# A three-layer graph network kernel: in layer 0 GpSimd instead of VectorE copies the gather indices of a pair

## The chip, the cores and the metric

The kernel runs on one core of one Trainium2 chip. The metric is the device time of one execution in microseconds; lower is better. Three executions of the kernel before took 4489.26, 4493.26 and 4494.06 us, with a median of 4493.26.

## The reference

A layer norm with ReLU in front, three rounds of mean aggregation over a graph (GraphSAGE), and the input added at the end. There are 100000 nodes of 128 features and 150000 edges sorted by destination, 100000 of them from a node to itself. The widths are 128, 256, 256 and 128; all is float32.

```python
def sage(h, w_self, w_neigh, b):
    agg = segment_sum(h[src], dst) * inv_deg
    return h @ w_self + agg @ w_neigh + b
h = jnp.maximum(_layernorm(x), 0.0)
h = relu(sage(h, ws0, wn0, b0))
h = relu(sage(h, ws1, wn1, b1))
return x + sage(h, ws2, wn2, b2)
```

## The kernel before, in words

The nodes are cut into tiles of 128, two tiles are a pair, and there are 392 pairs (`PAIRS`). A node's own edge to itself is added directly. The other edges of a tile, at most 128, have been put into a table in a preparation of about 200 us: `slot_index` holds for each tile and partition the source row to fetch, `slot_node` the place of its destination within the tile. A tile's sum over edges is then one gather of 128 rows and one matmul with a selection matrix. If the table does not hold all edges a flag leads to a general path (`general`); with these inputs it is not taken.

Each layer is a software pipeline in which every engine has its own program, and pair n is at another stage on each. `pipeline(eng, step, total, lag)` (line 83) calls `step` once per pair. Inside a step `first.back(k)` is the pair k places before, and it works in that pair's buffers. Buffers loaded from memory have 4 slots (`SLOTS`), most others 2 halves. Engines wait for each other with counting semaphores, and each queue is worked off in order. The order of the work within a step is written out by hand.

Layer 0, by engine, at the step of pair n:

- SyncE (`layer0_transfers`, lines 454 to 465) loads the pair's own rows of x into `raw[slot][:, 0:2]` as soon as pair n-4 is normalized (`L0.normed`), and stores the results P and Q of pair n-9.
- VectorE (`layer0`, line 1013) begins with `copies_index(L0, first)` (lines 978 to 985). It copies the two index columns of pair n from `slot_index` to `gather_at[slot]`, and adds one to `L0.index_copied`. Behind it, for pair n-1, it waits for the own rows and for both gathers (lines 1018 and 1019) and takes the statistics of four tiles (line 1021), then the selection matrix `select` (1026). There follow `self_scale` (1035), the moments (1039), `cat_lo` of pair n-4 (1047), `hid_lo` of pair n-6 (1055), Q of pair n-8 (1065), `rstd` (1073), the sum of own row and neighbours `agg` of pair n-2 (1082), its degree (1084), `shift` of pair n-1 (1088), `inv_degree` (1092) and P of pair n-7 (1099).
- GpSimd (`gathers`, lines 561 to 573) waits until pair n-4 is normalized, which frees the buffer, and until `L0.index_copied` is n+1; then it issues two indirect DMAs (line 569) that fetch 128 rows of x each into `raw[slot][:, 2:4]`.
- ScalarE (`layer0`, line 635) normalizes pair n-2 (line 649: two tiles of own rows, two of neighbours, then `L0.normed`), scales `agg` of pair n-3 (657), takes the square root for pair n-1 (663), the ReLU of pair n-5 (671), and `cat_hi` and `hid_hi` (679, 686).
- TensorE (`layer0`, line 1231) does the product of pair n-7 with the weights of the next layer (12 matmuls with 512 columns, `ps_out`), the sum matmuls of pair n-2 (line 1253, 4 matmuls, `ps_agg`), the transposes of pair n-3 (line 1264, which wait for `agg_ready` and for `cat_lo` of the pair before), and the product of pair n-4 (12 matmuls with 256 columns, `ps_hid`). Products are three terms of high and low parts, in `product` (line 1222).

Layer 1 has the same shape with other widths: `copies_index(L1, first)` is in VectorE's step there too, with a wait on the gathers of the slot's last use. Layer 2 works on groups of three tiles.

The lines that put the copy and the gathers in their order are these:

```python
def gather(s):
    if s.has(SLOTS):
        pool.wait_ge(freed, s.back(SLOTS).n + 1)
    pool.wait_ge(layer.index_copied, s.n + 1)
    pool.sem_inc(pool_may_go, 1)
    for j in range(2):
        pool.indirect_dma_start(...)
```

Of the kernel before, what the change touches and what calls it, by code (L numbers as in the profile page):

```python
# [16 lines left out]
D = 128  # L17
H = 256
PAIR = 2 * P
SLOTS = 4  # L20
PAIRS = -(-N_NODES // (PAIR * SLOTS)) * SLOTS
# [48 lines left out]
def peeled(step, first, last, total, slots=SLOTS):  # L70

    for n in range(first, last):
        step(Step(n // slots, n % slots, total, False, slots))


def looped(eng, step, first_use, last_use, total, slots=SLOTS):

    with eng.Fori(first_use, last_use) as i:
        for slot in range(slots):
            step(Step(i, slot, total, True, slots))  # L80


def pipeline(eng, step, total, lag, rounds=2, slots=SLOTS):

    assert lag < rounds * slots and total % slots == 0
    peeled(step, 0, rounds * slots, total, slots)
    looped(eng, step, rounds, total // slots, total, slots)
    peeled(step, total, total + lag, total, slots)


def build(nc, x, src, dst, windows, ws0, wn0, b0, ws1, wn1, b1, ws2, wn2, b2, out):
# [4 lines left out]
    h0_sums = nc.dram_tensor("h0_sums", [N_ROWS, D], FP32).ap()  # L96
# [9 lines left out]
    with ExitStack() as ctx:  # L106
        def sb(name, shape, dt=FP32):
            return ctx.enter_context(nc.sbuf_tensor(name, shape, dt))

        def sem(name):  # L110
            return ctx.enter_context(nc.semaphore(name))
# [23 lines left out]
        slot_index = sb("slot_index", [P, TILES], I32)  # L135
# [61 lines left out]
        raw = [t[:, :].rearrange("p (j f) -> p j f", j=4) for t in loaded_rows]  # L197
# [13 lines left out]
        gather_at = [sb(f"gather_at{i}", [P, SHARED], I32) for i in range(SLOTS)]  # L211
# [81 lines left out]
        tables_ready = sem("tables_ready")  # L293
# [53 lines left out]
        pool_may_go = sem("pool_may_go")  # L347

        L0, L1, L2 = Layer(0), Layer(1), Layer(2)
# [150 lines left out]
        def _(pool):  # L500
# [12 lines left out]
            for c in range(CHUNKS):  # L513
                pool.indirect_dma_start(win_mem[0:TP, c * 2 * WIN:(c + 1) * 2 * WIN], None, windows,
                                        bass.IndirectOffsetOnAxis(row_index[:, c:c + 1], axis=0),
                                        bounds_check=ROWS - 1, oob_is_err=False).then_inc(win_gathered, 16)
# [3 lines left out]
            last_row = pool.snap(limit)  # L520

            def general(pass_no):
                table, sums, width = GENERAL[pass_no]
                with pool.If(pool.value_load(general_flag[0:1, 0:1], min_val=0, max_val=1) != 0):
# [33 lines left out]
                    if pass_no == 0:  # L558
                        pool.wait_ge(ge_index_set, 1)

            def gathers(layer, table, rows_in, freed, width):
                def gather(s):
                    if s.has(SLOTS):
# [5 lines that stand above are left out]
                        pool.indirect_dma_start(rows_in[s.slot][:, j, 0:width], None, table,  # L569
                                                bass.IndirectOffsetOnAxis(gather_at[s.slot][:, j:j + 1], axis=0),  # L570
                                                bounds_check=last_row, oob_is_err=False
                                                ).then_inc(layer.gathered[s.slot], 16)
                pipeline(pool, gather, PAIRS, 0)

            def triple_gathers(s):
# [5 lines left out]
                for j in range(SHARED):  # L581
# [2 lines left out]
                                            bounds_check=last_row, oob_is_err=False  # L584
                                            ).then_inc(L2.gathered[s.slot], 16)

            pool.wait_ge(flag_set, 1)
            pool.wait_ge(nbr_cleared, SLOTS + 3)
            raw_nbr = [t[:, 2:4, :] for t in raw]
            general(0)  # L590
            with pool.If(pool.value_load(general_flag[0:1, 0:1], min_val=0, max_val=1) != 0):
                gathers(L0, h0_sums, raw_nbr, L0.normed, D)
            with pool.Else():
                gathers(L0, x, raw_nbr, L0.normed, D)

            for q in range(SLOTS):
                pool.memset(nbr[q][:, :, :], 0.0).then_inc(nbr_cleared, 1)
# [1 line left out]
            all_stored(pool, L0.stored, 2 * SLOT_USES)  # L599
            general(1)  # L600
            gathers(L1, p_dram, nbr, L1.summed, H)
            all_stored(pool, L1.stored, 2 * SLOT_USES)
            general(2)
# [149 lines left out]
        def _(dve):  # L753
# [221 lines left out]
                                          op1=ALU.add).then_inc(ge_nodes_set, 1)  # L975
                        dve.wait_ge(ge_nodes_set, 2)

            def copies_index(layer, s):

                if not s.live():  # L980
                    return
                if layer is not L0 and s.has(SLOTS):
                    dve.wait_ge(layer.gathered[s.slot], s.use * 32)
                dve.tensor_copy(gather_at[s.slot][:, 0:2], slot_index[:, bass.ds(s.n * 2, 2)]  # L984
                                ).then_inc(layer.index_copied, 1)

            def nbr_lo_part(layer, s, tiles, width):

                if not s.live():
                    return  # L990
                dve.wait_ge(layer.nbr_hi_ready, s.n + 1)
                if s.has(2):
                    dve.wait_ge(layer.summed, s.back(2).n + 1)
                dve.tensor_tensor(nbr_lo[s.half][:, 0:tiles, 0:width], nbr[s.slot][:, 0:tiles, 0:width],
                                  nbr_hi[s.half][:, 0:tiles, 0:width].bitcast(FP32), ALU.subtract
                                  ).then_inc(layer.nbr_split, 1)

            def means(layer, s, width, added):

                dve.wait_ge(layer.summed, s.n + 1)  # L1000
                if s.has(2):
                    dve.wait_ge(layer.turned, s.back(2).n + 1)
                for j in range(2):
                    last = dve.scalar_tensor_tensor(agg[s.half][:, j, 0:width],
                                                    row_sums[s.slot][:, j * H:j * H + width],
                                                    inv_degree[:, bass.ds(s.n * 2 + j, 1)],
                                                    added[:, j, 0:width], op0=ALU.mult, op1=ALU.add)
                last.then_inc(layer.agg_ready, 1)
# [2 lines left out]


            def layer0(first):
                copies_index(L0, first)
                t = first.back(1)
                if t.live():

# [23 lines left out]
                t = first.back(4)  # L1041
# [7 lines left out]
                t = first.back(6)  # L1049
# [7 lines left out]
                t = first.back(8)  # L1057
# [12 lines left out]
                t = first.back(1)  # L1070
# [3 lines left out]
                s = first.back(2)  # L1074
# [18 lines left out]
                t = first.back(7)  # L1093
# [9 lines left out]
            dve.wait_ge(nbr_cleared, SLOTS + 3)  # L1103
            dve.wait_ge(bias_loaded, 32)
            pipeline(dve, layer0, PAIRS, 8, rounds=3)

            general(1)


            def layer1(first):  # L1110
                copies_index(L1, first)
                nbr_lo_part(L1, first.back(4), L1_SPLIT, H)
                s = first.back(5)
                t = s.back(2)
                if t.live():

                    dve.wait_ge(L1.hi_ready, t.n + 1)
                    if t.has(2):
                        dve.wait_ge(L1.dense_done, t.back(2).n + 1)
                    dve.scalar_tensor_tensor(hid_lo[t.half][:, :, :],  # L1120
                                             l1_turn[t.half].rearrange("p (k n) -> p k n", k=2), 0.0,
                                             hid_hi[t.half][:, :, :].bitcast(FP32), op0=ALU.max, op1=ALU.subtract
                                             ).then_inc(L1.lo_ready, 1)
                t = s.back(4)
                if t.live():

                    dve.wait_ge(L1.z_ready, t.n + 1)
                    if t.has(SLOTS):
                        dve.wait_ge(L1.stored[t.slot], t.use * 32)
                    for j in range(2):  # L1130
                        last = dve.scalar_tensor_tensor(y_out[t.slot][:, j, :], z_out[t.slot][:, j, :],
                                                        self_scale[:, bass.ds(t.n * 2 + j, 1)],
                                                        l1_out[t.half][:, j * H + D:(j + 1) * H],
                                                        op0=ALU.mult, op1=ALU.add)
                    last.then_inc(L1.rows_ready, 1)
                if s.live():
                    dve.wait_ge(L1.own_loaded[s.slot], (s.use + 1) * 16)
                    means(L1, s, H, own[s.slot])
            pipeline(dve, layer1, PAIRS, 9, rounds=4)

            general(2)
# [238 lines left out]
```

## Time and profile before

| what | us |
|---|---|
| median of three executions | 4493.26 |
| the profiled execution | 4493.25 |
| its span, first to last instruction | 4491.1 |
| layer 0's gathers, first to last start | 199.9 to 2227.8 |
| layer 1's gathers, first to last start | 2264.1 to 3619.6 |
| layer 2's gathers, first to last start | 3640.5 to 4480.2 |
| TensorE busy | 3625.5 (81%) |
| VectorE busy | 3607.8 (80%) |
| ScalarE busy | 3057.1 (68%) |
| GpSimd busy | 2237.8 (50%) |

The profile calls the engines PE (TensorE matmuls), PEld (TensorE's weight loads), DVE (VectorE), ACT (ScalarE), POOL (GpSimd) and SP (SyncE). L984 is line 984 of the kernel. "<-" behind a group's idle time names what ended it. An instruction's duration reaches from its start to its last write, and the next one on the same engine may start before that; so durations on one engine can add up to more than the time that they fill. PEclk is TensorE's granted clock as a share of its full speed.

### The profile page before, as it was taken

What the parts mean: (1) busy time and instruction counts of PE and PEld (TensorE: products, weight loads), DVE (VectorE), ACT (ScalarE), POOL (GpSimd) and SP (SyncE); (2) the same over time, 40 slices, a digit from 0 to 9 for tenths busy, and PEclk for the clock granted to TensorE, in tenths of its full rate; (3) what the DMA queues carried; (4) which work ended last, traced back from release to release, by engine and by line L of the source; (5) the groups of instructions that cost most, each with busy time, mean ns of one, the idle gap of its engine ahead of it and who ended that gap; (6) DMA issues with size and microseconds to landing.
All of it is one profiled execution on the core that took longest, in us unless ns stands there. A gap on an engine that the chain in (4) does not pass through costs nothing. (4 is left out here: it accounts for less than half of the span.)

```text
span 4491.1 us, 111206 instructions
## 1 busy us (share of the span) xinstructions
PE 3625.5 (81%) x22512; PEld 3234.4 (72%) x22512; DVE 3607.8 (80%) x12979; ACT 3057.1 (68%) x7987; POOL 2237.8 (50%) x2122
## 2 busy tenths in 40 slices
PE   0199999999999999999978788777787765666565
PEld 0188888888888888888867677677677755555555
DVE  7899999999999999999956666666666666666666
ACT  0188888888888888888756666666666656666665
POOL 0144444444444444444355555555555556666665
PEclk9999999999999999999989999999999976665666
DMA  1044444444444444444456666666666667777777
GB/s 47 14 133 138 137 140 138 139 137 138 139 140 137 140 138 139 138 138 141 133 161 189 189 187 188 188 194 185 188 190 190 190 193 214 218 215 215 214 217 205
DMA packets 1040429, 726.89 MB, mean 162 GB/s; under 512 B 102859, under 2 KB 1012307, under 8 KB 1040303
## 3 DMA queue, kind: packets, MB, share of 16 engines
q1 hardware_dynamic: 854418, 569.79, 41.9%
q0 software_dynamic: 80384, 104.91, 9.6%
q10 hardware_dynamic: 105600, 51.92, 3.9%
q14 instruction: 21, 0.17, 0.0%
q8 instruction: 6, 0.10, 0.0%
HBM read 451.43 MB, written 360.72 MB: 181 GB/s over the span
## 5 line engine op out<-in xcount | busy, mean ns | idle before, releaser
L569 POOL DMA_INDIRECT loaded_rows<-in_x,gather_at x784 | 910.2, 1161 | 1263.4 <-DVE gather_at L984 1121.5
L1227 PE MATMUL ps_out<-w_hi,hid_hi 128*128 128x512 f32 (+1 forms) x3136 | 1111.5, 354 | 272.5 <-DVE hid_lo L1120 104.1
L569 POOL DMA_INDIRECT layer_mem<-p_rows,gather_at x784 | 787.9, 1005 | 601.6 <-issue 215.6
L1227 PE MATMUL ps_out<-w_lo,hid_hi 128*128 128x512 f32 (+1 forms) x3136 | 1065.7, 340 | 0.0
L1227 PE MATMUL ps_out<-w_hi,hid_lo 128*128 128x512 f32 (+1 forms) x3136 | 1060.2, 338 | 0.0
L1227 PEld LDWEIGHTS ps_out<-w_hi,hid_hi 128*128 128x128 f32 x3136 | 601.4, 192 | 421.9 <-issue 235.2
L582 POOL DMA_INDIRECT layer_mem<-z_rows,gather_at x528 | 527.3, 999 | 333.3 <-issue 154.8
L1227 PEld LDWEIGHTS ps_out<-w_hi,hid_lo 128*128 128x128 f32 x3136 | 600.9, 192 | 64.6
L1227 PEld LDWEIGHTS ps_out<-w_lo,hid_hi 128*128 128x128 f32 x3136 | 602.6, 192 | 50.3
L1120 DVE SCALAR_TENSOR_TENSOR hid_lo<-ps_out,hid_hi 128x512 fp32r<-128x512 f32 x392 | 270.6, 690 | 427.5 <-ACT hid_hi L727 351.2
L738 ACT ACTIVATE layer_mem<-iota_row,triple_node 128x128 f32<-128x128 f32 x1056 | 345.9, 391 | 272.9 <-issue 168.7
L1227 PE MATMUL ps_hid<-cat_hi,w_hi 128*128 128x256 f32 x1568 | 476.7, 304 | 0.0
L1227 PE MATMUL ps_hid<-cat_hi,w_lo 128*128 128x256 f32 x1568 | 445.2, 284 | 0.0
L1227 PE MATMUL ps_hid<-cat_lo,w_hi 128*128 128x256 f32 x1568 | 444.5, 283 | 0.0
L679 ACT ACTIVATE cat_hi<-ps_turn 128x512 fp32r<-128x512 f32 x392 | 234.6, 599 | 289.8 <-PE ps_turn L1264 285.5
L718 ACT ACTIVATE layer_mem<-ps_out 128x256 f32<-128x256 f32 x392 | 150.0, 383 | 391.3 <-DMA y_rows<-layer_mem 164.4
L1021 DVE BATCH_NORM_STATS2 stats<-loaded_rows 128x6 f32<-128x128 f32 x1568 | 341.2, 280 | 31.8 <-issue 12.3
L649 ACT ACTIVATE h_own<-loaded_rows,shift,rstd 128x128 f32<-128x128 f32 x784 | 342.1, 484 | 24.3 <-DVE shift L1088 14.1
L649 ACT ACTIVATE h_nbr<-loaded_rows,shift,rstd 128x128 f32<-128x128 f32 x784 | 340.6, 482 | 0.0
L1065 DVE SCALAR_TENSOR_TENSOR layer_mem<-stored_rows,self_scale,ps_out 128x256 f32<-128x256 f32 x784 | 339.3, 474 | 0.1
L671 ACT ACTIVATE layer_mem<-ps_hid,b_col 128x256 f32<-128x256 f32 x784 | 321.5, 460 | 1.1 <-DVE hid_lo L1055 0.7
L727 ACT ACTIVATE hid_hi<-ps_out 128x512 fp32r<-128x512 f32 x392 | 233.0, 594 | 109.5 <-PE ps_out L1322 87.5
(158 smaller groups left out, 8963.6 us busy)
## 6 DMA issues: line engine op xcount, KB each, us to landing
p_rows<-stored_rows SPq DMA_DIRECT2D x392, 256.0 KB
q_rows<-layer_mem SPq DMA_DIRECT2D x392, 256.0 KB
loaded_rows<-q_rows SPq DMA_DIRECT2D x392, 256.0 KB
loaded_rows<-y_rows SPq DMA_DIRECT2D x264, 192.0 KB
layer_mem<-in_x SPq DMA_DIRECT2D x264, 192.0 KB
out_rows<-stored_rows ACTq DMA_DIRECT2D x264, 192.0 KB
loaded_rows<-in_x SPq DMA_DIRECT2D x392, 128.0 KB
z_rows<-layer_mem SPq DMA_DIRECT2D x392, 128.0 KB
```

The source lines that it names most:

```text
L569: pool.indirect_dma_start(rows_in[s.slot][:, j, 0:width], None, table, bass.IndirectOffsetOnAxis(gather_at[s.slot][:, j:j + 1], axis=0), b ...
L582: pool.indirect_dma_start(triple_rows_in[s.slot][:, j, :], None, z_dram, bass.IndirectOffsetOnAxis(gather_at[s.slot][:, j:j + 1], axis=0), ...
L649: last = act.activation(rows, raw[t.slot][:, j, :], ACT.Relu, bias=shift[t.half][:, j:j + 1], scale=rstd[t.half][:, j:j + 1])
L671: last = act.activation(h1[t.half][:, m, :], ps_hid[t.half][:, m * PAIR:(m + 1) * PAIR], ACT.Relu, bias=b0_col[:, m:m + 1])
L679: act.activation(cat_hi[t.half][:, :, :], ps_turn[:, :].rearrange("p (k n) -> p k n", k=2), ACT.Copy).then_inc(L0.hi_ready, 1)
L718: act.activation(z_out[t.slot][:, :, :], l1_out[t.half].rearrange("p (j f) -> p j f", j=2)[:, :, 0:D], ACT.Copy).then_inc(L1.z_ready, 1)
L727: act.activation(hid_hi[t.half][:, :, :], l1_turn[t.half].rearrange("p (k n) -> p k n", k=2), ACT.Relu).then_inc(L1.hi_ready, 1)
L738: last = act.activation(triple_distance[s.half][:, b, :], iota_row[:, :], ACT.Abs, scale=-1.0, bias=triple_node[:, bass.ds(s.n * (2 * SHAR ...
L1021: last = dve.bn_stats(stats[t.half][:, j, :], raw[t.slot][:, j, :])
L1065: last = dve.scalar_tensor_tensor(q_out[t.slot][:, j, :], p_out[t.slot][:, j, :], self_scale[:, bass.ds(t.n * 2 + j, 1)], ps_out[t.half][: ...
L1120: dve.scalar_tensor_tensor(hid_lo[t.half][:, :, :], l1_turn[t.half].rearrange("p (k n) -> p k n", k=2), 0.0, hid_hi[t.half][:, :, :].bitca ...
L1227: ins = nc.tensor.matmul(o, a, b, start=n == 0, stop=n == len(terms) - 1)
```

## The change

In layer 0 the index copy leaves VectorE's step. GpSimd gets a step of its own, `layer0_gathers`, in place of `gathers`. At the step of pair n it waits until the gathers of pair n-4 have landed (the last to read that slot's `gather_at`) and copies the two index columns of pair n. Then, for pair n-1, it waits until pair n-5 is normalized and until its own copy of pair n-1 is done, and issues the two gathers. As it now reads `slot_index` itself, it waits once for `tables_ready` ahead of all. `copies_index` remains for layer 1 alone. Nothing else differs.

```diff
+            def layer0_gathers(table):
+                def step(first):
+                    if first.live():
+                        if first.has(SLOTS):
+                            pool.wait_ge(L0.gathered[first.slot], first.use * 32)
+                        pool.tensor_copy(gather_at[first.slot][:, 0:2], slot_index[:, bass.ds(first.n * 2, 2)]
+                                         ).then_inc(L0.index_copied, 1)
+                    s = first.back(1)
+                    if s.live():
+                        if s.has(SLOTS):
+
+                            pool.wait_ge(L0.normed, s.back(SLOTS).n + 1)
+                        pool.wait_ge(L0.index_copied, s.n + 1)
+                        pool.sem_inc(pool_may_go, 1)
+                        for j in range(2):
+                            pool.indirect_dma_start(raw[s.slot][:, 2 + j, :], None, table,
+                                                    bass.IndirectOffsetOnAxis(gather_at[s.slot][:, j:j + 1], axis=0),
+                                                    bounds_check=last_row, oob_is_err=False
+                                                    ).then_inc(L0.gathered[s.slot], 16)
+                pipeline(pool, step, PAIRS, 1)
...
+            pool.wait_ge(tables_ready, 1)
             pool.wait_ge(flag_set, 1)
             pool.wait_ge(nbr_cleared, SLOTS + 3)
-            raw_nbr = [t[:, 2:4, :] for t in raw]
             general(0)
             with pool.If(pool.value_load(general_flag[0:1, 0:1], min_val=0, max_val=1) != 0):
-                gathers(L0, h0_sums, raw_nbr, L0.normed, D)
+                layer0_gathers(h0_sums)
             with pool.Else():
-                gathers(L0, x, raw_nbr, L0.normed, D)
+                layer0_gathers(x)
...
-            def copies_index(layer, s):
+            def copies_index(s):
 
                 if not s.live():
                     return
-                if layer is not L0 and s.has(SLOTS):
-                    dve.wait_ge(layer.gathered[s.slot], s.use * 32)
+                if s.has(SLOTS):
+                    dve.wait_ge(L1.gathered[s.slot], s.use * 32)
                 dve.tensor_copy(gather_at[s.slot][:, 0:2], slot_index[:, bass.ds(s.n * 2, 2)]
-                                ).then_inc(layer.index_copied, 1)
+                                ).then_inc(L1.index_copied, 1)
...
             def layer0(first):
-                copies_index(L0, first)
                 t = first.back(1)
...
             def layer1(first):
-                copies_index(L1, first)
+                copies_index(first)
```

## Rows read from the trace of the kernel before

**Rows 1.** Busy time by stretch, layers 0 and 1: `us, busy (x)` per engine, clock, DMA.

```profile
303.80:2199.50 1895.70, 1880.29 (x11647) 1676.88 (x11646) 1850.28 (x7645) 1547.60 (x4005) 848.62 (x728) 1.00 0.45 139
2300.00:3500.00 1200.00, 956.77 (x6923) 867.53 (x6921) 819.65 (x2416) 750.78 (x2072) 692.73 (x690) 0.97 0.66 188
```

**Rows 2.** Group of the index copy, VectorE, 300 to 2200 us: busy, mean | idle.

```profile
L984 DVE COPY gather_at<-slot_index 128x2 int32 x365 | 57.9, 159 | 0.0
```

**Rows 3.** Waits, 300 to 2200 us: engine, line, releaser, total us, times, longest.

```profile
POOL loaded_rows L569 <- DVE gather_at L984: 923.6, 364, 4.9
...
PE ps_turn L1264 <- DVE cat_lo L1047: 14.2, 7, 2.1
```

**Rows 4.** Timeline, layer 0, three pairs: start, us, engine, line, what, count [idle before].

```profile
1005.61 0.87 ACT L649 ACTIVATE h_nbr<-loaded_rows,shift,rstd 128x128 f32<-128x128 f32 x2
...
1005.64 0.16 DVE L984 COPY gather_at<-slot_index 128x2 int32 x1
...
1006.60 1.20 POOL L569 DMA_INDIRECT loaded_rows<-in_x,gather_at  x1 [2.38 <-DVE gather_at L984]
...
1007.84 0.68 DVE L1055 TENSOR_TENSOR hid_lo<-layer_mem,hid_hi 128x512 fp32r<-128x512 f32 x1
...
1008.11 1.29 POOL L569 DMA_INDIRECT loaded_rows<-in_x,gather_at  x1 [0.30 <-issue]
...
1010.72 0.16 DVE L984 COPY gather_at<-slot_index 128x2 int32 x1
...
1010.97 0.87 DVE L1021 BATCH_NORM_STATS2 stats<-loaded_rows 128x6 f32<-128x128 f32 x4
...
1012.99 1.00 POOL L569 DMA_INDIRECT loaded_rows<-in_x,gather_at  x1 [0.30 <-issue]
...
1015.97 0.16 DVE L984 COPY gather_at<-slot_index 128x2 int32 x1
1016.03 0.87 DVE L1021 BATCH_NORM_STATS2 stats<-loaded_rows 128x6 f32<-128x128 f32 x4
...
1021.05 0.16 DVE L984 COPY gather_at<-slot_index 128x2 int32 x1
```

**Rows 5.** Timeline around one late gather, layer 0.

```profile
483.57 1.00 POOL L569 DMA_INDIRECT loaded_rows<-in_x,gather_at  x1 [1.86 <-issue]
...
486.56 0.61 PE L1253 MATMUL ps_agg<-h_nbr,select 128*128 128x130 f32 x4
486.98 0.87 DVE L1021 BATCH_NORM_STATS2 stats<-loaded_rows 128x6 f32<-128x128 f32 x4 [2.10 <-issue]
...
489.31 0.37 PE L1264 MATMUL ps_turn<-ident,h_own 128*128 128x128 f32 x1 [2.14 <-DVE cat_lo L1047]
```

**Rows 6.** Busy time and granted clock (PEclk) just behind that gather.

```profile
489.30:492.80 3.50, 3.49 (x17) 3.50 (x18) 3.45 (x14) 2.79 (x7) 0.00 (x0) 0.52 0.31 104
```

**Rows 7.** Timeline, layer 0, starts of the sum matmuls and of the copy.

```profile
495.49 0.61 PE L1253 MATMUL ps_agg<-h_nbr,select 128*128 128x130 f32 x4
...
502.84 0.16 DVE L984 COPY gather_at<-slot_index 128x2 int32 x1
...
533.81 0.16 DVE L984 COPY gather_at<-slot_index 128x2 int32 x1
...
536.02 0.61 PE L1253 MATMUL ps_agg<-h_nbr,select 128*128 128x130 f32 x4
```

**Rows 8.** GpSimd's groups over the whole span: busy, mean | idle before.

```profile
L569 POOL DMA_INDIRECT loaded_rows<-in_x,gather_at x784 | 910.2, 1161 | 1263.4 <-DVE gather_at L984 1121.5 <-issue 141.3 <-ACT h_nbr L649 0.6
...
L502 POOL IOTA iota_col_i<- 128x1 int32 x1 | 0.1, 128 | 0.0
...
L510 POOL MEMSET inv_degree<- 128x8 f32 x1 | 0.1, 95 | 0.0
```

**Rows 9.** Timeline, layer 0, a gather that starts ahead of a two-input subtraction.

```profile
868.34 1.00 POOL L569 DMA_INDIRECT loaded_rows<-in_x,gather_at  x1 [0.31 <-issue]
868.43 0.68 DVE L1055 TENSOR_TENSOR hid_lo<-layer_mem,hid_hi 128x512 fp32r<-128x512 f32 x1
```
## The prediction, made before the changed kernel was built or run

> **What bounds the kernel now.** I read the busy table by stretch first. In layer 0 TensorE is busy 1880.3 of 1895.7 us and VectorE 1850.3; in layer 1 both are far lower [rows 1]. So layer 0 has two engines that can each set the pace, and the sum depends on which one waits for the other. The change touches layer 0 alone, so the question is what one pair costs there. VectorE's copy of the indices ran 365 times between 303.8 and 2199.5 us [rows 1, 2], which is 1895.7 / 364 = **5.208 us a pair**.
>
> Next the timeline of three pairs, to see whether VectorE runs freely [rows 4]. Its copies start at 1005.64, 1010.72, 1015.97 and 1021.05: steps of 5.08, 5.25 and 5.08. In the long step the statistics of the pair before start 0.25 us behind the copy (1010.72 to 1010.97), in the short one behind it 0.06 (1015.97 to 1016.03). What differs is GpSimd. The gathers that those statistics need were issued one step earlier. For the long step the second one is written out by 1008.11 + 1.29 = 1009.40, and the statistics start 1.57 later; for the short one by 1012.99 + 1.00 = 1013.99, which leaves 2.04. So a gather's rows land about 1.57 us after it was written out, and the whole way from the copy (1005.64) over GpSimd's two gathers to the statistics (1010.97) is 5.33 us: as long as a step. When the second gather takes 1.29 it is late, when it takes 1.00 it is not. VectorE shows hardly any idle time for this, since the copy's own 0.16 us covers the gap.
>
> The gather is much later now and then. At 483.57 one starts after 1.86 us in which nothing released it, the statistics start 2.10 us late, and TensorE's transposes then wait 2.14 us for VectorE's cat_lo [rows 5]. The list of waits has 7 of these, 14.2 us in sum [rows 3]. Behind this one TensorE's granted clock was 0.52 over 3.5 us [rows 6], that is its lower level of 1.2 GHz for nearly all of it, so from one sum matmul (486.56) to the next (495.49) it took 8.93 us [rows 5, 7].
>
> Last, TensorE's own pace. After that event it is behind, VectorE is not yet in its way, and its sum matmuls start at 495.49 and, eight pairs on, at 536.02 [rows 7]: 40.53 / 8 = **5.067 us a pair**. In that time VectorE went from 502.84 to 533.81 in six pairs, 5.16 each [rows 7]. So TensorE, left alone, needs 5.067; VectorE and the gathers make it 5.208.
>
> **The change, part by part.** (1) *VectorE's copy goes.* 392 copies of 0.159 us [rows 2], but the next instruction can start 0.06 us behind a copy [rows 4], so its place in VectorE's queue is worth 0.06 us a pair. A step without a late gather took 5.08 with the copy [rows 4], so about 5.02 without. That is under TensorE's 5.067 and stops counting there.
>
> (2) *The gathers' start moves from VectorE's step to ScalarE's.* GpSimd now waits for normed of the pair that last held the buffer, and for its own copy of a step earlier. At the step whose copy starts at 1005.64 (pair k), ScalarE ends the normalization of pair k-2 at 1005.61 + 0.87 = 1006.48 [rows 4]. That frees the buffer of pair k+2, whose statistics come three steps later, near 1010.97 + 2 x 5.17 = 1021.3. From release to use there are then 14.8 us, and the way from the gather's start (1006.60) to its use (1010.97) needs 4.37. Ten us are spare. The ordinary lateness of 0.2 us and the rare one of 2.1 both fit in, so I take both as gone, the clock's dips behind them too. The lead comes from the wait on normed; the copy one pair ahead only keeps it off the gather's path. The own rows' load by SyncE has had the same wait on normed all along, so it is as early as the gathers will be, and I count nothing for it as the next to be late. What is late next is TensorE's own queue.
>
> (3) *GpSimd's added copy, and its wait on gathered.* No copy on GpSimd is in this trace. From below, its smallest instructions: 0.095 and 0.128 us [rows 8]. From above: VectorE's 0.16 plus a whole hid_lo of 0.68 in front of it, 0.84. I take 0.13, as its size is nearest the small ones. The gather that its wait names was issued three pairs earlier, so that wait costs nothing. Per pair GpSimd then has: copy 0.13; the way from a release to the first gather 0.80 (copy's end 1005.80 to 1006.60); two gathers from 1006.60 to 1009.40, 2.80 [rows 4]. Sum 3.73, at worst 4.44, under 5.067 either way: off the path. Queued behind the copy are only the gathers, ten us early. If that cover were gone the copy would cost its own 0.13 to 0.84.
>
> (4) *What GpSimd does to VectorE.* The first gathers land in other places of VectorE's step. When VectorE's hid_lo (two operands in SBUF) began before a gather, the gather took 1.29 us [rows 4]; when the gather began 0.09 before it, hid_lo kept its 0.68 and the gather its 1.00 [rows 9]. So gathers give way and do not hold VectorE up. A copy could hold it up by its own length, 0 to 0.13. VectorE's slack of 0.05 a pair takes part of it; I take 0.
>
> The Trainium skill (page "SBUF — State Buffer", section "Who interferes with whom") says that a VectorE instruction with two SBUF inputs and a GpSimd instruction that reads SBUF block each other, the later one for the whole of the earlier. By that rule hid_lo in rows 9 would have waited the gather's 1.00 us, and a pair could cost up to 1 us more; the trace agrees only for the gather that waits. It is the rule that speaks against this change.
>
> (5) *The wait on tables_ready* is met together with flag_set: nothing. Layers 1 and 2 keep their instructions, and the first pairs gain a us or so, not counted.
>
> The sum: a pair goes from 5.208 to TensorE's 5.067, rounded to 5.07 for a stray wait: 392 x 0.138 = 54 us. The profiled execution took 4493.25 us, its span 4491.1, the median of the runs 4493.26, so no correction: 4493 - 54 = **4439**.
>
> **The rivals.** *VectorE keeps the pace.* Its step of 5.08 may keep the copy's 0.06 as work of its sequencer, and GpSimd's copy may hold up select or hid_lo by 0.07 to 0.13: 5.15 to 5.21. At 5.15: 4493 - 392 x 0.058 = 4470. For it: VectorE is 97.6% busy [rows 1] and its slack is only 0.05. Against it: rows 9.
>
> *The gathers stay late.* If GpSimd's queue (copy of the next pair first, with a wait on gathered) kept it from running ahead, the landing would stay where it is: 4493. Against it: that wait names a gather three pairs old.
>
> *GpSimd becomes the bound: slower.* The place is GpSimd's new copy, between two pairs of gathers. If it can't start until the gathers before it have landed, it costs 1.57 more: 0.80 + 2.80 + 1.57 + 0.13 = 5.30 a pair, (5.30 - 5.208) x 392 = 36 us, 4529. It decides from 5.21 - 3.60 = 1.6 us for the copy and what it waits for. For it: no ordinary instruction stands between gathers in this trace. Against it: the second gather starts 0.30 behind the first without waiting for its landing [rows 4].
>
> *More than forecast.* TensorE's 5.067 may be shortened where the transposes follow closer: under 4430.
>
> **How the numbers follow.** Forecast 0.68, VectorE's pace 0.16, gathers still late 0.05, GpSimd the bound 0.07, more 0.04. A measurement of this kernel can tell some 0.2%, 9 us, from no change. The forecast's own spread is 5.06 to 5.10 a pair, 4435 to 4451. The range runs from 4430 to 4476, which takes in that and most of VectorE's case: 0.8. Faster by over 0.2%: forecast, more and nearly all of VectorE's case, 0.87; within: 0.06; slower: 0.07.
>
> **What would show it.** Right: in layer 0 the sum matmuls 5.07 apart, no wait of the transposes for cat_lo near 2 us, gathers that start after normed and some ten us before their statistics, GpSimd's copy near 0.1 us, clock at 1.00 throughout, VectorE idle rising as it now waits for TensorE. Wrong: VectorE's statistics still ended by a gather's landing; a GpSimd copy over 1.4 us; select or hid_lo starting late; or layers 1 and 2 of another length.

## The result, and the profile after

The changed kernel takes 4440.8 us in the median (4437.4 to 4443.63), the kernel before 4493.47 in runs beside it: the ratio is 0.9882, with a 95% interval of 0.987 to 0.9893. That is 53 us less, where 54 were forecast.

The sum matmuls' row of the view by tile (form, count, duration in ns as min/median/max, first and last start) gives layer 0's length. Before, it read 207.9 to 2237.9 us. After:

```profile
L1273 PE MATMUL ps_agg<-h_nbr,select x1568: 272/274/559, 208.3 to 2188.1; 128*128 128x130 f32 x196
```

So layer 0 went from 2030.0 to 1979.8 us, 50.2 less, over 391 steps from 5.192 to 5.063 each. The other 2 to 3 us lie in layer 1, whose gathers span 1348 us in this execution and 1353 in another of the same kernel, against 1355 before.

The busy table by stretch, over the same part of layer 0 and over layer 1, answers to [rows 1]:

```profile
303.80:2146.50 1842.70, 1842.70 (x11639) 1664.80 (x11638) 1821.63 (x7277) 1509.37 (x4002) 872.71 (x1091) 1.00 0.47 143
2300.00:3500.00 1200.00, 955.13 (x6945) 861.97 (x6944) 824.78 (x2430) 755.03 (x2082) 699.66 (x696) 0.98 0.68 190
```

TensorE is busy in every microsecond of this stretch of layer 0. That alone would not show that it sets the pace: the first experiment below has the same full share at a slower one. The list of waits from 300 to 2140 us, whole, answers to [rows 3]; no wait of TensorE or VectorE is left in it:

```profile
POOL loaded_rows L576 <- ACT h_nbr L670: 835.7, 355, 2.4
ACT cat_hi L700 <- PE ps_turn L1284: 333.1, 363, 0.9
POOL loaded_rows L576 <- issue: 129.9, 371, 2.6
```

The timeline answers to [rows 4]. GpSimd is now released by ScalarE's normalization:

```profile
999.96 0.87 ACT L670 ACTIVATE h_nbr<-loaded_rows,shift,rstd 128x128 f32<-128x128 f32 x2
...
1001.66 1.20 POOL L576 DMA_INDIRECT loaded_rows<-in_x,gather_at  x1 [2.38 <-ACT h_nbr L670]
...
1002.16 0.61 PE L1273 MATMUL ps_agg<-h_nbr,select 128*128 128x130 f32 x4
...
1003.17 1.00 POOL L576 DMA_INDIRECT loaded_rows<-in_x,gather_at  x1 [0.30 <-issue]
...
1004.16 0.20 POOL L566 COPY gather_at<-slot_index 128x2 int32 x1
...
1007.23 0.61 PE L1273 MATMUL ps_agg<-h_nbr,select 128*128 128x130 f32 x4
...
1014.38 0.86 DVE L1041 BATCH_NORM_STATS2 stats<-loaded_rows 128x6 f32<-128x128 f32 x4
```

The normalization that ends at 1000.83 frees the buffer, the gathers start at 1001.66, and the statistics that use them come at 1014.38: 12.7 us, of which some 4 are needed. Sum matmuls are 5.07 apart. GpSimd's copy shows 0.20 us.

The late gather is still there, seven times in layer 0. This is one of them, in the same view:

```profile
1016.86 1.19 POOL L576 DMA_INDIRECT loaded_rows<-in_x,gather_at  x1 [2.28 <-ACT h_nbr L670]
...
1017.36 0.61 PE L1273 MATMUL ps_agg<-h_nbr,select 128*128 128x130 f32 x4
...
1019.97 1.00 POOL L576 DMA_INDIRECT loaded_rows<-in_x,gather_at  x1 [1.91 <-issue]
...
1022.43 0.61 PE L1273 MATMUL ps_agg<-h_nbr,select 128*128 128x130 f32 x4
```

The second gather starts 1.91 us behind the end of the first, where 0.30 is the usual, as in [rows 5], and the matmuls keep their 5.07.

### The profile page after: what moved, and what is told of

Its sections match the earlier page's. It is cut to its first block and busy times, and to the rows that moved or that the text cites. A ratio compares the mean times of both kernels' runs of the same rounds, so it can differ in the third digit from the quotient of the medians.

```text
span 4435.0 us, 111303 instructions
## 1 busy us (share of the span) xinstructions
PE 3592.3 (81%) x22512; PEld 3226.0 (73%) x22512; DVE 3579.0 (81%) x12587; ACT 3019.0 (68%) x7987; POOL 2268.4 (51%) x2514
## 5 line engine op out<-in xcount | busy, mean ns | idle before, releaser
L576 POOL DMA_INDIRECT loaded_rows<-in_x,gather_at x784 | 863.0, 1101 | 1029.4 <-ACT h_nbr L670 888.3
```

What stands on the lines that cost most here:

```text
L576: pool.indirect_dma_start(raw[s.slot][:, 2 + j, :], None, table, bass.IndirectOffsetOnAxis(gather_at[s.slot][:, j:j + 1], axis=0), bounds_ ...
```

## The experiments

The theory was that the gain is the gathers' lead. The rival was that it is VectorE's instruction gone. The first four runs ran on a chip where the kernel before takes 4035.4 us: layers 1 and 2 are shorter there (layer 1's gathers span 1050 us), while layer 0 seems to be the same: the run with pair k-3 takes 5.058 us a pair there, the changed kernel 5.063 on the other. I compare each run with the kernel before on its own chip, and layer 0 by the sum matmuls' first and last start.

**VectorE keeps the copy, two pairs ahead** (on the kernel before):

```diff
-            def layer0(first):
-                copies_index(L0, first)
+            def layer0(ahead):
+                copies_index(L0, ahead)
+                first = ahead.back(2)
...
-            pipeline(dve, layer0, PAIRS, 8, rounds=3)
+            pipeline(dve, layer0, PAIRS, 10, rounds=3)
```

> VectorE keeps its index copy, but makes it two pairs ahead; GpSimd's gathers are as before. Theory (the gain is the gathers' lead): they start when normed frees the buffer and are off VectorE's way. VectorE's step is 5.08 us with its copy and no late gather, TensorE's 5.067, so a pair takes 5.07 to 5.08: 4440 to 4447 us, gathers released by normed. Rival (the gain is VectorE's instruction gone): no more than the late landings are saved, VectorE still sets the pace: 4465 to 4490.

Measured: 4001.75 us against 4035.41, ratio 0.9918 (0.9901 to 0.9934), 34 us less; layer 0 208.2 to 2205.1, a pair 5.107. The lead alone gives two thirds of the gain, less than the theory said and more than the rival allowed. The busy table from 300 to 2200 us and all of VectorE's waits in that time:

```profile
300.00:2200.00 1900.00, 1899.88 (x11879) 1703.23 (x11878) 1868.29 (x7795) 1626.60 (x4085) 737.13 (x742) 1.00 0.46 141
...
DVE inv_degree L1093 <- DVE degree L1085: 8.4, 46, 0.2
DVE inv_degree L1093 <- issue: 8.3, 46, 0.2
```

TensorE's share is full, yet at 5.107 us a pair it is held back, as it can do 5.067; VectorE waits for no other engine. The timeline of VectorE:

```profile
999.33 0.69 DVE L1100 TENSOR_TENSOR stored_rows<-ps_out,b_rows 128x512 f32<-128x512 f32 x1
...
1004.12 0.15 DVE L1089 SCALAR_TENSOR_TENSOR shift<-moments,rstd 128x4 f32<-128x4 f32 x1
...
1004.46 0.17 DVE L1093 RECIPROCAL inv_degree<-degree 128x2 f32 x1 [0.18 <-DVE degree L1085]
...
1004.63 0.69 DVE L1100 TENSOR_TENSOR stored_rows<-ps_out,b_rows 128x512 f32<-128x512 f32 x1
...
1009.38 0.15 DVE L1089 SCALAR_TENSOR_TENSOR shift<-moments,rstd 128x4 f32<-128x4 f32 x1
...
1009.58 0.17 DVE L1093 RECIPROCAL inv_degree<-degree 128x2 f32 x1
...
1009.70 0.69 DVE L1100 TENSOR_TENSOR stored_rows<-ps_out,b_rows 128x512 f32<-128x512 f32 x1
```

From P to P VectorE takes 5.30 us in one pair and 5.07 in the next, with no late gather in either. From 300 to 2130 us every fourth step is one of 5.30 or 5.31 (the loop in `pipeline` holds four pairs), and the other three take 5.04 to 5.08. So VectorE sets the pace here. But 0.13 us of the long step lies between the starts of shift and inv_degree (0.34 against 0.20 in the next), where the kernel before never has more than 0.22. That is 0.03 us a pair, some 12 us in layer 0, that only this version shows; why it does stays open. So the 34 us may understate what the lead is worth with the copy left on VectorE.

**The copy on GpSimd, without the lead** (on the changed kernel, as the next two):

```diff
                             pool.wait_ge(L0.normed, s.back(SLOTS).n + 1)
+                        if s.has(8):
+                            pool.wait_ge(L0.p_ready, s.back(8).n + 1)
...
-                pipeline(pool, step, PAIRS, 1)
+                pipeline(pool, step, PAIRS, 1, rounds=3)
```

> The changed kernel, but the gathers of pair k also wait until VectorE has made P of pair k-8, which is where VectorE's copy stood: the copy is gone from VectorE, the lead too. Theory: a loop over two pairs comes back. From P's start to the statistics that need the gather 0.69 + 0.80 + 4.37 = 5.86 us, from those statistics to the next P 4.5; 10.3 / 2 = 5.15 a pair, and the seven rare late gathers cost their 2 us and the clock's dips again: 4470 to 4490. Rival: 4440, as the copy is gone from VectorE.

Measured: 4019.6 us, ratio 0.9962 (0.9948 to 0.9976), 16 us less; layer 0 208.4 to 2224.8, a pair 5.157, where the loop's sum said 5.15 (its two terms, 5.86 and 4.5, make 5.18). Its waits from 300 to 2200 us:

```profile
POOL loaded_rows L578 <- DVE stored_rows L1121: 879.6, 366, 4.7
...
DVE stats L1043 <- DMA loaded_rows<-in_x,gather_at: 29.1, 79, 2.4
...
PE ps_turn L1286 <- DVE cat_lo L1069: 14.4, 7, 2.2
```

With the copy gone from VectorE its wait for the gathers stands in the open, and the seven stalls of TensorE are back with 14.4 us, as in [rows 3]. Neither half alone gives the 50 us: they gave 34 and 16.

**Less lead.** The gathers wait for a later pair's normalization, here k-2; the next run has 3 in place of 2:

```diff
-                        if s.has(SLOTS):
+                        if s.has(2):
 
-                            pool.wait_ge(L0.normed, s.back(SLOTS).n + 1)
+                            pool.wait_ge(L0.normed, s.back(2).n + 1)
```

> The changed kernel, but the gathers of pair k wait until pair k-2 is normalized (not k-4): ten us less lead. Theory: a loop over two pairs, normed to gather's start 0.8, to the statistics 4.37, from those to shift 4.3, to normed 1.8 to 2.4: 11.3 to 11.9 over two pairs, 5.6 to 5.9 a pair: 4650 to 4780 us, slower than the kernel before. Rival: 4440.

Measured: 4126.54 us, ratio 1.0232 (1.0215 to 1.0249), 91 us more; layer 0 208.1 to 2331.5, 5.430 a pair. The loop is there, shorter than I had made it:

```profile
1000.34 0.87 DVE L1041 BATCH_NORM_STATS2 stats<-loaded_rows 128x6 f32<-128x128 f32 x4 [0.36 <-DMA loaded_rows<-in_x,gather_at]
...
1004.41 0.15 DVE L1108 SCALAR_TENSOR_TENSOR shift<-moments,rstd 128x4 f32<-128x4 f32 x1
...
1005.39 0.87 ACT L670 ACTIVATE h_nbr<-loaded_rows,shift,rstd 128x128 f32<-128x128 f32 x2
...
1007.09 1.02 POOL L576 DMA_INDIRECT loaded_rows<-in_x,gather_at  x1 [2.80 <-ACT h_nbr L670]
...
1010.97 0.87 DVE L1041 BATCH_NORM_STATS2 stats<-loaded_rows 128x6 f32<-128x128 f32 x4 [0.31 <-DMA loaded_rows<-in_x,gather_at]
```

Shift's end (1004.56) to normed (1006.26) 1.70, to the gather 0.83, to the statistics 3.88, and from statistics (1000.34) to shift's end (1004.56) another 4.22: 10.63 over two pairs, 5.32 each. My 4.37 from gather to statistics was one with both gathers stretched. The rest to 5.43 goes for the most part to the rare late gathers, which nothing hides here: from 300 to 2320 us the median step of the statistics is 5.34, and fifteen steps of 6.2 to 7.9 us, fourteen of them within 20 us of a late gather, hold 30 us more than that. So the time was 91 us over the kernel before, not 157 to 287.

> The same with pair k-3: five us less lead, the same loop over three pairs, 3.8 to 4.0 a pair, under TensorE's 5.067: no change, 4437 to 4445 us. Five us are spare, so the rare late gather of 2 us stays hidden too. Rival (the lead works in degrees): 4450 to 4480.

Measured: 3984.97 us, ratio 0.9876 (0.986 to 0.9893), as the changed kernel; layer 0 208.2 to 2185.9, a pair 5.058. One pair more in the loop, and the lead is enough: between two and three pairs lies a threshold, and a fourth adds nothing.

**The changed kernel again**, on a chip with the long layer 1:

> The changed kernel once more, beside experiments. On a chip where layers 1 and 2 are shorter by some 455 us, as in the first four experiments, the gain should be the same 50 us in layer 0 and the ratio 0.987 to 0.988: near 3984 us where the kernel before takes 4035; where it takes 4493, 4441.

Measured: 4442.12 us against 4493.78, ratio 0.988 (0.9864 to 0.9897).

**More small copies on GpSimd**, four, twelve and twenty-four per pair, behind the index copy:

```diff
+                    if first.live():
+                        if first.has(1):
+                            pool.wait_ge(extra_done, first.n)
+                            pool.sem_inc(pool_may_go, 1)
+                        for r in range(4):
+                            last = pool.tensor_copy(wf_key_mem[:, 2 * r:2 * r + 2], ones[:, 0:2])
+                        last.then_inc(extra_done, 1)
```

> The changed kernel with four more small copies on GpSimd per pair of layer 0, behind its index copy. In the changed kernel GpSimd's copy ends at 1004.36 and the next release comes at 5.93: 1.57 us free in a pair. Four copies of 0.19 us and a further wait take 0.8 to 1.2 of that: no change against the changed kernel within 0.2%, a pair stays at 5.067. Rival (a small copy on GpSimd costs far more than its record shows): 5.2 and more a pair, over 50 us slower than the changed kernel.

> The changed kernel with twelve more small copies on GpSimd per pair of layer 0. With four of them each took 0.13 us of the queue, and 1.07 us a pair were left (1.91 before a gather, of which 0.84 are the way from a release to it). Eight more take 1.0: just in, so 5.07 to 5.10 a pair, 0 to 15 us slower than the changed kernel. Rival (small reads hold VectorE's two-input instructions up): slower in proportion, 30 us and more.

> The same with twenty-four. GpSimd's queue then holds 2.5 us of gathers, 25 copies of 0.13 and a start of 0.3 to 0.8: 6.0 to 6.5 a pair, over TensorE's 5.067, so GpSimd is the bound and each pair is 0.9 to 1.4 us longer: 360 to 560 us slower than the changed kernel. This is the rival that the prediction called GpSimd the bound, brought about on purpose.

Measured: 4440.89 us with four, 4443.11 with twelve, 4757.69 with twenty-four. GpSimd's rows, with twelve:

```profile
1004.17 0.20 POOL L567 COPY gather_at<-slot_index 128x2 int32 x1
...
1004.29 1.71 POOL L574 COPY wf_key_mem<-ones 128x2 f32<-128x2 f32 x12
...
1005.04 0.87 ACT L678 ACTIVATE h_nbr<-loaded_rows,shift,rstd 128x128 f32<-128x128 f32 x2
...
1006.75 1.21 POOL L584 DMA_INDIRECT loaded_rows<-in_x,gather_at  x1 [0.74 <-issue]
```

and with twenty-four:

```profile
1000.65 3.16 POOL L574 COPY wf_key_mem<-ones 128x2 f32<-128x2 f32 x24
...
1003.96 1.02 POOL L584 DMA_INDIRECT loaded_rows<-in_x,gather_at  x1 [0.15 <-POOL wf_key_mem L574]
...
1005.29 0.99 POOL L584 DMA_INDIRECT loaded_rows<-in_x,gather_at  x1 [0.31 <-issue]
...
1009.78 1.02 POOL L584 DMA_INDIRECT loaded_rows<-in_x,gather_at  x1 [0.15 <-POOL wf_key_mem L574]
```

With twelve the copies end about when the release comes (1005.91, the end of the normalization), and the gather still starts 0.84 us behind it, as in the changed kernel. So they just fill the time in which GpSimd would have waited, and layer 0's steps stay at 5.063 us; its first gather starts 5 us later. With twenty-four GpSimd's queue is 5.82 us long (1003.96 to 1009.78), and that is the pace. So a copy costs the queue 0.13 us, and the 1.6 us a pair of twelve are free in it. The step with twenty-four I had put at 6.0 to 6.5, as I counted 0.3 to 0.8 for the next gather's start; behind a copy it is 0.15. The time was some 317 us over the changed kernel's, not 360 to 560.

**One long piece of work on GpSimd**, a copy of 128 x 1024 numbers, and a memset of the same size, in the same place:

```diff
-                        for r in range(4):
-                            last = pool.tensor_copy(wf_key_mem[:, 2 * r:2 * r + 2], ones[:, 0:2])
-                        last.then_inc(extra_done, 1)
+                        pool.tensor_copy(wf_key_mem[:, 0:1024], w_hi[:, 0:4, :].rearrange("p k n -> p (k n)").bitcast(FP32)).then_inc(extra_done, 1)
```

> The changed kernel with one long copy on GpSimd per pair, 128 x 1024 numbers from SBUF to SBUF, behind the index copy: 1.0 to 1.5 us from about 4.4 us of a step that begins at 0, when VectorE runs P, the statistics, select and more. Theory (GpSimd's reads do not hold VectorE up, as a gather ahead of hid_lo did not): select and hid_lo keep their starts, 5.067 a pair, no change against the changed kernel. Rival (two SBUF inputs on VectorE block with an ordinary GpSimd read for its whole length): select starts or ends 0.4 to 1.0 us late in each pair, a pair takes 5.3 to 5.9, 100 to 330 us slower. The kernel does this added copy for its time alone.

> The same place and length, but a memset of 128 x 1024, which reads nothing from SBUF; a memset of 128 x 512 took 0.54 us, so this takes about 1.1. Both theories: no change against the changed kernel, 5.067 a pair. If this one is slower too, the length of GpSimd's work matters and not what it reads.

Measured: with the memset the time is the changed kernel's, 4440.0 us. The copy takes 4828.73 us, ratio 1.074 (1.0722 to 1.0758). The timeline with the copy:

```profile
1001.12 1.48 DVE L1114 SCALAR_TENSOR_TENSOR shift<-moments,rstd 128x4 f32<-128x4 f32 x1
...
1001.40 0.20 POOL L567 COPY gather_at<-slot_index 128x2 int32 x1
...
1001.53 1.05 POOL L573 COPY wf_key_mem<-w_hi 128x1024 f32<-128x1024 f32 x1
...
1002.52 0.15 DVE L1118 RECIPROCAL inv_degree<-degree 128x2 f32 x1
...
1002.64 0.88 ACT L676 ACTIVATE h_own<-loaded_rows,shift,rstd 128x128 f32<-128x128 f32 x2 [1.48 <-DVE shift L1114]
```

and with the memset:

```profile
1004.19 0.96 POOL L573 MEMSET wf_key_mem<- 128x1024 f32 x1
...
1004.96 0.41 DVE L1052 TENSOR_TENSOR select<-iota_row,slot_node 128x256 fp32r<-128x256 f32 x1
...
1006.63 1.24 POOL L582 DMA_INDIRECT loaded_rows<-in_x,gather_at  x1 [1.48 <-ACT h_nbr L676]
```

In seven steps of the run with the copy, behind a rare late gather, the copy meets select in place of shift:

```profile
522.10 1.75 DVE L1052 TENSOR_TENSOR select<-iota_row,slot_node 128x256 fp32r<-128x256 f32 x1
...
522.53 1.04 POOL L573 COPY wf_key_mem<-w_hi 128x1024 f32<-128x1024 f32 x1
```

My theory fell here. Shift reads moments and rstd, two operands in SBUF. Its record is 0.15 us long in the other kernels; here it is 1.48 and ends with GpSimd's copy (1002.58 against 1002.60). The rival had named select and hid_lo; it was the next instruction of the same kind that was hit, and select only in those seven steps. The pair takes 6.05, more than the 5.3 to 5.9 of the rival. Length alone does not do it: the memset of 0.96 us, which reads nothing, ran beside select 354 times from 300 to 2130 us, and select, with two operands in SBUF, stayed at 0.41 at most. (Select began behind the memset and ahead of the copy, so the two cases differ in order too.) The memset was not without any effect: behind each of the seven late gathers self_scale's record reaches to the memset's end, 1.44 to 1.52 us in place of 0.22 to 0.38, but nothing waited for it.

The Trainium skill (page "SBUF — State Buffer", section "Who interferes with whom") says that a VectorE instruction with two SBUF inputs contends with a GpSimd instruction that reads SBUF, not with one that only writes it. The two runs agree for shift and select (1.48 and 1.75 us with the copy, 0.41 for select with the memset); why it is so they do not show.

**Layer 1's copy on GpSimd too** (on the changed kernel):

```diff
-                def gather(s):
+                def gather(first):
+                    if first.live():
+                        if first.has(SLOTS):
+                            pool.wait_ge(layer.gathered[first.slot], first.use * 32)
+                        pool.tensor_copy(gather_at[first.slot][:, 0:2], slot_index[:, bass.ds(first.n * 2, 2)]
+                                         ).then_inc(layer.index_copied, 1)
+                    s = first.back(1)
+                    if not s.live():
+                        return
...
-                pipeline(pool, gather, PAIRS, 0)
+                pipeline(pool, gather, PAIRS, 1)
...
             def layer1(first):
-                copies_index(first)
```

> The changed kernel with layer 1's index copy moved to GpSimd in the same way. Where layer 1 takes 1350 us (3.45 a pair) GpSimd's two gathers at 1.30 fill 2.6 of it, so a copy of 0.13 to 0.5 has room: no change against the changed kernel, within 10 us. Where layer 1 takes 1050 us (2.69 a pair) GpSimd's gathers follow each other without a gap, so the copy adds its time: 2.75 to 3.1 a pair, 25 to 160 us slower than the changed kernel. Rival: as in layer 0 the lead helps, 20 us or more faster.

> The kernel with layer 1's index copy on GpSimd too, once more and in more rounds, as it came out 12 us faster than the changed kernel where its expectation said within 10. If that is real, the ratio to the kernel before is again near 0.986 where layer 1 takes some 1350 us, and layer 1's gathers span 10 to 17 us less than the changed kernel's 1348 to 1353. If it falls to a chip with a layer 1 of 1050 us, GpSimd's queue is full there and the ratio comes out over the changed kernel's 0.9876: 0.994 or more.

Measured: 4428.96 us, ratio 0.9861 (0.9845 to 0.9878), and again 4427.46, ratio 0.9861 (0.9844 to 0.9877), both where the kernel before takes 4490. Layer 1's gathers span 1335 and 1334 us, against 1348 to 1353 in the changed kernel. So this version is faster than both, by about 12 us against the changed kernel's 4441; the intervals of the two ratios overlap, and it rests on the spans and on the repeat. What a chip with the short layer 1 makes of it wasn't measured. There the gathers of the runs above follow each other at 1.30 us, so I would expect a loss.

## Why the prediction was right

**The sum** was 54 us and the runs gave 53, and that it came so close is in part luck. It multiplied a step of 5.208, read in the middle of the layer, by all 392 pairs. Over the whole layer the step was 5.192, so layer 0 gave 50.2 us, and 2 to 3 us came from layer 1, which was put at nothing.

**TensorE's pace as the floor** was right to the third digit. It came from eight pairs behind a stall [rows 7], the one place where TensorE ran without being held up, and in the changed kernel four steps from 1002.16 to 1022.43 make 5.068 each.

**The lead.** The 14.8 us from release to use are 13.6 in the trace (1000.83 to 1014.38), enough by far, and the run with pair k-3 shows that five less would do. The rare late gathers were hidden and the clock's dips with them: in the kernel before, windows of some 3.5 us behind the first, third, sixth and seventh late gather read 0.51 to 0.53, and in the changed kernel windows of 20 us around all seven read 1.00. (A mean over the whole layer cannot show this; it reads 1.00 in both.) The seven waits of 14.2 us are gone.

**The copy's place in VectorE** is open by some hundredths. The prediction gave VectorE 5.08 with the copy and 5.02 without. In the one version that has the copy and no late gather it takes 5.12 from 300 to 2130 us, of which 0.03 is seen in that version alone. The 5.08 was read off two of the shorter steps. That version gained 16 us less than the changed kernel; up to 12 of them may be its own. The forecast was not hurt, since both values without the copy lie under TensorE's 5.067.

**GpSimd's copy** was put at 0.13 us of its queue and costs that, though its record is 0.19 to 0.20. The queue with it was put at 3.73 us and takes 3.46, as only one of the two gathers is stretched; 1.6 us stay free.

**What GpSimd does to VectorE** was taken as nothing, and it is nothing, but the reason given was only half right. A gather does not hold back hid_lo, which has two SBUF inputs: that rested on one case [rows 9], and from 300 to 2130 us 101 gathers of the kernel before and 358 of the first experiment start ahead of hid_lo and overlap it; hid_lo takes 0.68 in the mean and the gather 1.00. Where hid_lo is first (239 gathers of the kernel before) the gather takes 1.29. A long ordinary copy does hold such an instruction back. The copy of the change does not because it is short, and because it does not meet one: in 354 of 361 pairs it runs beside P and the statistics, and neither has two SBUF inputs. With twelve small copies more, some run beside select in each pair, and select takes 0.44 at most in place of 0.41.

**Of the rivals**, VectorE at 5.15 did not come, and GpSimd as the bound needs more than the 1.6 us of further work that twelve copies are. I estimate 2.4: twenty-four copies are 24 x 0.13 = 3.1 us, less the 5.82 - 5.07 by which they overran. The prediction had 1.6 for it, as it counted 0.80 for the way from a release and 2.80 for the two gathers; in the full queue these are 0.15 and 2.31 (1003.96 to 1006.27).

## What to carry to other kernels

Where an engine prepares something for another and uses the result a step later, add up the way round the loop and divide by the pairs in it: here 5.33 us for a step of 5.2 looked like no wait at all, since the preparing instruction's own record covered the gap. Start the transfer from the event that frees its buffer. Read an engine's own pace where it was left alone, as behind a stall, over several steps; single steps flatter where, as here, every fourth is a longer one. Small copies can go to GpSimd; a long one that reads SBUF costs VectorE its time where it meets an instruction with two SBUF inputs, here 0.98 us a pair for a copy of 1.04.

## What the runs showed of the hardware

The late gather comes by count and not by time. In the kernel before, the pairs of gathers with a late second one start at 480.5, 761.7 and 1042.7 us, 281 apart, in the changed kernel at 469.7, 743.3 and 1016.9, 273.6 apart: 54 pairs, that is 108 gathers, in both. With the 5.43 us a pair of the run with pair k-2 they are 293.2 us apart in the mean, 54 pairs again. What happens in GpSimd at every 108th gather stays open.

Two chips gave 4035 and 4490 us for the same kernel. Layer 0, bound by TensorE and by the loop, showed no difference that these runs could tell (no kernel was profiled on both); layer 1 takes 1050 us of gathers on one and 1350 on the other, at 245 and 188 GB/s from 2300 to 3000 us (the run with pair k-3, and the kernel before). A profile taken on one need not name the bound of layer 1 on the other.
